# One-hots compared with a ramp in PSUM instead of one in SBUF, in a graph network kernel that gathers by indirect DMA

## What is computed

```python
h = relu(layernorm(x)); msg = relu(h[src]);                x += mlp(h + segment_sum(msg, dst))
h = relu(layernorm(x)); 4 times: a = segment_sum((h @ W[k] + b[k])[etypes, src], dst); h = gru(a, h);  x += h
h = relu(layernorm(x)); twice: h = segment_sum(norm * (h @ W)[src], dst) + b  (relu between);          x += h
h = relu(layernorm(x)); e = W @ [h[dst], h[src] - h[dst]] + b; e = leaky(batchnorm(e));  x += segment_mean(e, dst)
```

## Time and profile before

| | us |
|---|---|
| timed runs, median (lowest to highest) | 18841.41 (18836.34 to 18843.33) |
| profiled execution, span | 21319.6 |
| POOL busy | 13832.9 (65%) |
| TensorE busy | 10388.0 (49%) |
| VectorE busy | 4301.6 (20%) |
| ScalarE busy | 813.3 (4%) |

### The profile page before, as it was taken

How to read it: one execution, slowest core, us unless ns; L and a number is a source line. 1 busy time by engine, 2 the same in 40 slices (tenths; PEclk the granted TensorE clock), 3 DMA queues, 4 the chain that set the end, 5 groups by cost and what they waited for, 6 DMA issues and landing times.

```text
span 21319.6 us, 182142 instructions
## 1 busy us (share of the span) xinstructions
PE 10388.0 (49%) x40885; PEld 8431.9 (40%) x40886; DVE 4301.6 (20%) x4825; ACT 813.3 (4%) x2691; POOL 13832.9 (65%) x13640
## 2 busy tenths in 40 slices
PE   3333544445444463444634445443544445666689
PEld 2333333334333343333433333333433334656678
DVE  2111121112111121111211113111211112111168
ACT  0000000001000010000100001000000000000000
POOL 6766557774677746777377764676567764666677
PEclk5555555555555555555555555555555555555555
DMA  1111011110111111111111100111011111222222
GB/s 40 22 22 22 17 40 22 23 22 28 29 23 23 23 35 22 22 23 23 35 22 23 23 21 18 22 23 23 21 23 23 23 22 35 66 66 66 66 63 64
DMA packets 739325, 656.19 MB, mean 31 GB/s; under 512 B 457733, under 2 KB 467541, under 8 KB 738918
## 3 DMA queue, kind: packets, MB, share of 16 engines
q0 software_dynamic: 407168, 419.46, 9.4%
q1 hardware_dynamic: 332134, 236.47, 3.9%
HBM read 532.79 MB, written 122.26 MB: 31 GB/s over the span
## 4 chain that ended last, share of the span: by engine, by line
POOL 36%; another core or an unknown queue 25%; issue 19%; PE 15%; DVE 3%; DMA 1%; DVEq 1%; ACT 1%; POOLq 0%; ACTq 0%; SPq 0%
POOL HG L479 30%; PE ps L722 7%; POOL HG L461 5%; PE ps L875 2%; PE ps L803 2%; PE ps L719 1%; DVE OH L1012 1%; PE ps L766 1%; DMA HG<-tab_edge,STG 1%; PE ps L866 1%; DVEq L1005 1%; PE ps L835 0%; ACT RZ L643 0%; DMA HG<-tab_gin,STG 0%
## 5 line engine op out<-in xcount | busy, mean ns | idle before, releaser
L722 PE MATMUL ps<-HG,OH 128*128 (+2 forms) x26560 | 6212.0, 421 | 5999.6 <-issue 2938.7
L722 PEld LDWEIGHTS ps<-HG,OH 128*128 128x128 f32 x26560 | 5859.6, 329 | 6909.3 <-issue 6907.0
L479 POOL DMA_INDIRECT HG<-tab_gated,STG x6252 | 6424.0, 1028 | 2729.0 <-issue 2037.4
L479 POOL DMA_INDIRECT HG<-tab_gcn,STG x3126 | 3192.7, 1021 | 1386.1 <-issue 942.1
L1008 DVE TENSOR_TENSOR A<-A,ps 128x640 f32 (+1 forms) x1328 | 1091.9, 822 | 14010.3 <-issue 13934.3
L719 PE MATMUL ps<-ZERO 1*128 1x512 bf16 (+1 forms) x3819 | 1543.4, 535 | 3677.8 <-issue 2629.8
L461 POOL DMA_INDIRECT HG<-tab_gin,STG x1660 | 1712.9, 1032 | 750.3 <-issue 514.8
L461 POOL DMA_INDIRECT HG<-tab_edge,STG x1660 | 1587.9, 957 | 879.0 <-issue 490.4
L719 PEld LDWEIGHTS ps<-ZERO 1*128 1x128 bf16 x3819 | 338.8, 114 | 4260.3 <-issue 4199.7
L1012 DVE TENSOR_TENSOR OH<-IOTAR,DLOC 128x1280 f32<-128x1280 f32 x1328 | 2002.5, 1508 | 0.3 <-DVE A L1130 0.2
L875 PE MATMUL ps<-A,HG 128*128 (+1 forms) x3320 | 733.8, 353 | 601.6 <-issue 493.8
(11 more groups left out here) (157 smaller groups left out, 3002.8 us busy)
## 6 DMA issues: line engine op xcount, KB each, us to landing
HG<-tab_gated,STG POOLq DMA_INDIRECT x6252
A<-dloc_dram SPq DMA_DIRECT2D x166, 320.0 KB
kept<-HG SPq DMA_DIRECT2D x166, 320.0 KB
HG<-kept SPq DMA_DIRECT2D x166, 320.0 KB, 2.9
tab_gated<-TW SPq DMA_DIRECT2D x196, 256.0 KB, 2.0
HG<-tab_gcn,STG POOLq DMA_INDIRECT x3126
HG<-tab_gin,STG POOLq DMA_INDIRECT x1660
HG<-tab_edge,STG POOLq DMA_INDIRECT x1660
```

The lines of the kernel that those rows point to most:

```text
L479: nc.gpsimd.indirect_dma_start(out=RINGF[:, at:at + D], out_offset=None, in_=table, in_offset=bass.IndirectOffsetOnAxis(ap=STG[:, h, u:u + ...
L722: return nc.tensor.matmul(ps[:, base:][:, bass.ds(place, width)], onehots_, rows_, start=False, stop=False, skip_group_check=True)
```

## The change

The ramp is copied once, at the start, into the last 128 columns of PSUM, and the compare reads it there. So the compare has one input in PSUM and one (`DLOC`) in SBUF, where it had two in SBUF. The PSUM of the last stage's odd groups moves from column 3072 to column 0. All else is the same.

```diff
+SUM_AT = [2048, 0]
...
-        ps_s = ps[:, 2048:4096].rearrange("p (h u f) -> p h u f", h=2, f=D)
+        ps_s = [ps[:, at:at + GRP * D].rearrange("p (u f) -> p u f", f=D) for at in SUM_AT]
+        ps_ramp = ps[:, 4096 - P:4096]
...
-                base = 2048 + 1024 * h
+                base = SUM_AT[h]
...
             dve.wait_ge(iota_done, 4)
+            V.tensor_copy(ps_ramp, IOTAR[:, :])
...
-                return V.tensor_tensor(OH[:, h, :, :], IOTAR[:, :].unsqueeze(1).broadcast_to([P, GRP, P]),
+                return V.tensor_tensor(OH[:, h, :, :], ps_ramp.unsqueeze(1).broadcast_to([P, GRP, P]),
                                        cols.unsqueeze(2).broadcast_to([P, GRP, P]), ALU.is_equal)
...
-                add_group(LAST_PASS, g, ps_s[:, h, :, :], D)
+                add_group(LAST_PASS, g, ps_s[h], D)
```

## The result

The changed kernel takes 18366.89 us (median of 4 runs, 18365.9 to 18367.21), the kernel before 18842.37 (4 runs): ratio 0.9748, 95% interval 0.9734 to 0.9762. That is 475 us less, where 551 were forecast (18,290 us). The profiled execution of the changed kernel spans 18364.8 us, the same as its timed runs, so its profile can be read without carrying anything over.

A forecast was written before the change was run, and what follows sets the result against it. The prediction took POOL, issuing indirect DMAs and held up by compares, to bound the passes. From 18,841 us it took 546 for the compares' hold and 5 for the last stage: 18,290 us, range 17,830 to 18,610.

The forecast's parts named there:

- the next gather's stop: In the passes: a gather runs 0.13 us, then stands until the compare ends and does its other 0.82 us.
- 1162 x 0.47 = 546 us: Gain in the seven passes: 1162 compares beside gathers, each taken to cost 0.47 us of hold.
- three handles: Three estimates of one compare's price in the passes: 0.17 to 0.43, 0.54 and 0.75 us; 0.47 was taken.
- The single row: One compare in the second pass's timeline, placed 0.44 us into a gather: a price of 0.54 us.
- The mean over the first profile: Excess of gather means over medians in the profiled execution: 872 us together, 0.75 us a compare.
- The balance: Timed median less gathers at 1.251 us and time outside the passes: leaves 0.17 to 0.43 us a compare.
- The compare's duration: The compare with its ramp in PSUM was expected to take 1.48 us, as with two SBUF inputs.
- The last stage: TensorE is full there, so little of POOL's freed 1.0 us a group counts: 0 to 27 us, 5 taken.
- R1: Rival: TensorE paces the passes, so at most a third of 546 us is gained, 18,660 to 18,800 us; chance 0.08.
- R2: Rival: the compare still holds POOL, or never was what held it; 18,841 us, within 0.2%; chance 0.05.
- R3: Rival: TensorE stands while VectorE reads the ramp in PSUM, 246 us in the last stage; 18,889 us; chance 0.02.
- R4: Rival: compares fall badly in the timed runs' cycle, 0.9 us or more each; 17,390 to 17,795 us; chance 0.07.

The follow-up runs named there:

- e1: The changed kernel with the ramp of the seven passes back in SBUF, the last stage's still in PSUM: 18853.57 us, ratio 0.9993 to the kernel before.
- e6: The changed kernel with the compare's two inputs exchanged, DLOC first and the ramp in PSUM second: 18369.50 us, ratio 0.9751 to the kernel before.
- e5: The changed kernel plus an unused copy of 896 PSUM columns between add and compare in the passes: 18369.24 us, ratio 0.9750 to the kernel before.
- e4: As e1, plus an unused copy of 896 PSUM columns that delays each compare by 1.00 us: 19290.77 us, ratio 1.0226 to the kernel before.
- e9: The kernel before, unchanged, run and profiled once more: 18860.74 us (one run), profiled span 18858.9 us.
- e7: The changed kernel with the eighth pass's compare made a tensor_tensor against a column in PSUM: 18331.90 us, ratio 0.9731 to the kernel before.
- e3: As e1, plus an unused copy of 384 PSUM columns that delays each compare: 19343.15 us, ratio 1.0254 to the kernel before.

## Why the prediction was right

**The mechanism held.** A compare with both inputs in SBUF holds the gather that starts under it until it is over; with the ramp in PSUM it doesn't. Shown by e1 (back in SBUF, back to 996 ns), e6 (either order is free) and e5 (no price at other places). L1130's one row was enough evidence for the new form.

**One step of it was wrong, without harm.** "the next gather's stop would be reached 0.13 us into that gather" put the edge of the price 0.13 us behind the gather's start, with prices from 0.23 us to "nearly all of its 1.48". It lies about 0.03 us ahead of the start, and the prices go from 0.13 to 1.33 us (e4). The forecast took its price from a place of 0.44 us, where the edge doesn't matter; over all the 1148 compares of e9 that can be placed, the recorded edge would give 622 us, and they measure 468. The expectation of e4 hung on the edge, and missed.

**The size was off by a seventh.** The term was "1162 x 0.47 = 546 us". It measures about 462 us by the timed gain of 475 less the last stage's 13, and 477 by the profile of e9, on a chip where the timed gain is 492. Of the three handles, two were one-sided. The single row gave 0.54, and stood for one compare of many; e9 has such a one at place 0.44, but the mean place of its compares is 0.31. The mean over the first profile gave 0.75: there only 289 of 994 compares that can be placed in a cycle start in its first 0.5 us, in e9 1020 of 1148. That the start isn't random in a pass without waits carried the forecast: with 0.75 it would have been 17,965 us. That is still inside the range, so the range doesn't prove this point; the 477 us do.

**The balance was the best handle, partly by luck.** It gave "(197 + 300) / 1162 = 0.43 us". By the traces of the first profile and of e9, what lies outside the passes shrank by 271 us and not 300 (2723 to 2452; the last add of the second pass comes 11 us behind the last gather, where it was 57). The cycle is 1.2483 us in e9 and not 1.251, some 34 us over 12,698 gathers. And the balance put the stretches of the eighth pass at nothing, though that pass had them too, some 36 us (e7). The three nearly cancel: 197 + 271 + 34 - 36 = 466 us, 0.40 each. The 0.47 itself was a choice between 0.43 and 0.54, and no row gave it.

**The compare's duration**, 1.48 us expected, is 1484 ns. **The last stage** was put at 5 us of 0 to 27, and is 13; L526 fell to 1.54 us as expected, and TensorE, being full, kept nearly all of it. **The copy of the ramp** shows in nothing.

**The rivals.** R1 (TensorE paces the passes) is out: e9 and the changed kernel have no wait of POOL in a pass but for the first gather's. The argument against it, that the waits must belong to the profiled execution, was right, but its sum (2165 us of 2478) left 313 us open and took no account of the compares' own price, which was higher there. By the pages and traces of the two executions of the kernel before, the 2461 us between them are 1788 of POOL's idle time between gathers, 402 of longer gathers and 271 outside the passes. R2 is out by the result. R3: the zeroes (0.71 us) and products (4.53) are the same under a compare that reads PSUM. R4: a place as bad as 0.9 us and more was made by e3 and e4, and isn't the kernel's own.

## What to carry to other kernels

When GpSimd issues indirect DMAs back to back and is the bound, look for gathers whose duration is over the median and for the VectorE instruction that runs at that moment; moving one of its two inputs to PSUM freed 0.41 us for each here at no cost, and even a form 0.6 us slower on VectorE was a gain. Price such a hold by where it falls in the gather cycle, over all the instructions of the loop and not by one of them, and not by its mean in a profile whose span is far from the timed runs. Before relying on such a profile, take its waits off and see whether the balance gives the timed runs.

## What was not expected of the hardware

- The price of one compare runs from 0.13 to 1.33 us, rises by one us for each us that it starts later in the cycle of 1.25 us, and falls back for a compare that starts less than about 0.03 us ahead of the next gather (e4). Work of 0.47 us put on an engine that idles 80% of the time cost 490 us in e3, and work of 1.0 us nothing in e5.
- The kernel before differs by chip (18,841 to 18,866 us) where the changed one, measured on fewer of them, doesn't (18,367 to 18,370). That the places of the compares shift with the landing of the gathers would explain it, and isn't shown.
- One execution under the profiler took 2461 us longer than another of the same kernel (21319.6 and 18858.9), with TensorE's products drawn apart while gathers ran. What slowed it isn't known.
- One gather of 8.5 us at the start of the first pass stood long before the compare that it goes away with. Why isn't known.
